# A two-layer graph network on one core: PE's signals given by drains instead of by matmuls

## What is computed

```python
# layer 0
scores = where(A != 0, -arange(N), -inf);  vals, idx = top_k(scores, 25)
agg = X[idx].max(over the 25);  agg = maximum(agg, 0) where degree <= 25
x = layernorm(x + relu(concat(x, agg) @ W + b))
# layer 1 (adjacency is 0/1, so one edge type is live)
h = x @ W1;  e_src, e_dst = h . a_src, h . a_dst          # per head
w = leaky_relu(e_src[i] + e_dst[j]) where adj, else -1e9
out = relu(softmax(w) @ h + bias) + h
x = layernorm(x + headwise_layernorm(out) * gamma + beta)
```

## Time and profile before

| | us |
|---|---|
| median of 3 runs (lowest to highest) | 6567.95 (6542.93 to 6576.8) |
| the profiled execution | 6569.77 |
| its span | 6568.0 |

### The profile page before, as it was taken

The page is one execution under the profiler, slowest core; times in us unless marked ns, Lnnn a source line. Parts: engine busy times, 40 slices in busy tenths (PEclk is TensorE's granted clock), DMA queues, the critical chain, the costliest instruction groups (busy, mean ns, idle before and its releaser), DMA issues.

```text
span 6568.0 us, 57561 instructions
## 1 busy us (share of the span) xinstructions
PE 3758.1 (57%) x12546; PEld 1690.9 (26%) x12546; DVE 3914.1 (60%) x12445; ACT 2183.1 (33%) x4674; POOL 3318.6 (51%) x3204
## 2 busy tenths in 40 slices
PE   1222456656556556556566556566556656555687
PEld 1111222322222222223222222222222222222232
DVE  4544565665665665666566556566556656656666
ACT  3333223333333333333333333333333333333212
POOL 4666555455455455455555545545545555554500
PEclk9555667677777777776777767777767777777888
DMA  4433333333333333333333333333333333333200
GB/s 125 122 115 115 105 100 105 103 100 109 105 99 110 99 105 106 107 96 105 100 106 109 100 102 108 100 105 104 104 98 105 103 102 107 104 102 98 78 21 26
DMA packets 264399, 658.75 MB, mean 100 GB/s; under 512 B 62161, under 2 KB 128978, under 8 KB 247762
## 3 DMA queue, kind: packets, MB, share of 16 engines
q0 software_dynamic: 153600, 419.64, 22.1%
q1 hardware_dynamic: 110546, 236.66, 10.3%
HBM read 605.73 MB, written 50.33 MB: 100 GB/s over the span
## 4 chain that ended last, share of the span: by engine, by line
another core or an unknown queue 26%; DVE 24%; PE 24%; issue 20%; ACT 5%; DVEq 1%; POOL 1%; DMA 0%; SPq 0%; ACTq 0%; POOLq 0%
PE acc L1253 11%; DVE uv L832 7%; PE pB L1221 5%; DVE rmax L851 3%; DVE top L719 3%; PE acc L1179 2%; DVE key_b L721 2%; PE pB L1222 1%; ACT raw L569 1%; PE pT L1153 1%; PE pB L1237 1%; DVE rmax L860 1%; DVE key_a L721 1%; DVE stf L953 1%
## 5 line engine op out<-in xcount | busy, mean ns | idle before, releaser
L492 POOL DMA_INDIRECT rows<-in_x_dram,idx x3200 | 3318.4, 1037 | 2891.7 <-DVE rmax L851 1693.3
L1253 PE MATMUL acc<-uv,hs 128*65 128x512 f32 x4096 | 2156.8, 683 | 172.5 <-ACT raw L569 171.5
L832 DVE SCALAR_TENSOR_TENSOR uv<-rq,qinv,maskT 128x512 f32<-128x512 f32 x2048 | 1504.4, 741 | 1175.5 <-remote 674.0
L1221 PE MATMUL pB<-w_sb,xaT 128*128 128x256 f32 x1024 | 443.9, 608 | 1305.6 <-DVE pad L734 794.6
L1253 PEld LDWEIGHTS acc<-uv,hs 128*65 128x65 f32 x4096 | 622.5, 159 | 1440.8 <-issue 1396.9
L634 ACT ACTIVATE xaT<-pA 128x512 f32<-128x512 f32 x128 | 76.4, 597 | 2071.6 <-remote 1788.3
L1221 PEld LDWEIGHTS pB<-w_sb,xaT 128*128 128x128 f32 x1024 | 300.6, 308 | 1469.0 <-issue 1012.8
L732 DVE SCALAR_TENSOR_TENSOR key_b<-pB,wordkey 128x128 f32<-128x128 f32 x128 | 36.7, 287 | 914.7 <-remote 834.0
L851 DVE TENSOR_TENSOR rmax<-rmax,rows 128x1280 f32<-128x1280 f32 x384 | 569.7, 1484 | 7.0 <-DMA rows<-in_x_dram,idx 4.4
L1231 PE MATMUL pA<-id,xh 128*128 128x128 f32 x256 | 81.6, 418 | 811.7 <-DVE xh L814 432.9
L643 ACT ACTIVATE x1T<-pA 128x256 f32<-128x256 f32 x128 | 49.2, 384 | 1089.5 <-PE pA L1231 979.2
(11 more groups left out here) (116 smaller groups left out, 4509.4 us busy)
## 6 DMA issues: line engine op xcount, KB each, us to landing
adj_sb<-in_adj_dram SPq DMA_DIRECT2D x128, 1024.0 KB
rows<-in_x_dram,idx POOLq DMA_INDIRECT x3200
xh_dram<-xh SPq DMA_DIRECT2D x128, 256.0 KB
xr<-xh_dram SPq DMA_DIRECT2D x64, 512.0 KB
xt<-in_x_dram SPq DMA_DIRECT2D x128, 128.0 KB
out_dram<-xr SPq DMA_DIRECT2D x32, 512.0 KB, 2.9
w_sb<-in_L_gnn_W_dram SPq DMA_DIRECT2D x1, 512.0 KB
wcat<-in_L_gnn_W_dram SPq DMA_DIRECT2D x2, 128.0 KB
```

The source lines that it names most:

```text
L492: nc.gpsimd.indirect_dma_start(rows[:, c, r * C:(r + 1) * C], None, x_rows, bass.IndirectOffsetOnAxis(ap=idx[u][:, k:k + 1], axis=0)).then ...
L832: stt = nc.vector.scalar_tensor_tensor(uv[k][:, i, :], rq[i][:], inv, m, ALU.max, ALU.mult)
L1221: nc.tensor.matmul(p_lin, xaT[:, c, :], w0_sb[:, c, :], start=(c == 0), stop=False)
L1253: last = nc.tensor.matmul(acc[i][0:HW, :], hs[:, (1 - quad.par) * JT + jt, h, :], uv[k][:, i, :], start=(jt == 0), stop=(jt == JT - 1))
```

## The change

Nine signals of PE's loops move. Where the last matmul of a group incremented the group's semaphore, now a drain instruction stands behind it and increments it. Matmuls, their order and all waits stay. The signal of the small check at the program's end (L1291) and the branch behind it are unchanged.

```diff
--- before.py
+++ after.py
@@ -1150,8 +1150,8 @@
                         pe.wait_ge(s_ring, v)
                     for j in range(HALF):
                         jt = hf * HALF + j
-                        last = nc.tensor.transpose(pT[hf][:, j * P:(j + 1) * P], mask_sb[:, jt * P:(jt + 1) * P], id16[:])
-                    last.then_inc(s_T, 1)
+                        nc.tensor.transpose(pT[hf][:, j * P:(j + 1) * P], mask_sb[:, jt * P:(jt + 1) * P], id16[:])
+                    pe.drain().then_inc(s_T, 1)
 
             def pack_words(quad, u, g_of):
 
@@ -1164,8 +1164,8 @@
                 for v in quad.reach(lambda q: QT * q + u + g_of - FRONT):
                     pe.wait_ge(s_proj, v)
                 for jt in range(JT):
-                    last = nc.tensor.matmul(p_key[:, jt * WPT:(jt + 1) * WPT], stage[:, jt, :], pack[:], start=True, stop=True)
-                last.then_inc(s_key, 1)
+                    nc.tensor.matmul(p_key[:, jt * WPT:(jt + 1) * WPT], stage[:, jt, :], pack[:], start=True, stop=True)
+                pe.drain().then_inc(s_key, 1)
 
             def back(quad, pair):
 
@@ -1176,9 +1176,9 @@
                 for i in range(QT):
                     for h in range(PAIR):
                         at = (i % 2 * PAIR + h) * HW
-                        last = nc.tensor.matmul(acc[i // 2][:, at:at + HW], sT[:, h, i * P:(i + 1) * P],
+                        nc.tensor.matmul(acc[i // 2][:, at:at + HW], sT[:, h, i * P:(i + 1) * P],
                                                 backmat[:, PAIR * pair + h, :], start=True, stop=True)
-                last.then_inc(s_back, 1)
+                pe.drain().then_inc(s_back, 1)
 
             def broadcast(quad, pair):
 
@@ -1188,9 +1188,9 @@
                     pe.sem_inc(s_go["pe"], 1)
                 block = (quad.q - BQ) % BQ * IB
                 for i in range(PAIR):
-                    last = nc.tensor.matmul(rq[i][:], headsel[:, PAIR * pair + i, :],
+                    nc.tensor.matmul(rq[i][:], headsel[:, PAIR * pair + i, :],
                                             er[0:HEADS, bass.ds((1 - quad.par) * N + block, IB)], start=True, stop=True)
-                last.then_inc(s_rq, 1)
+                pe.drain().then_inc(s_rq, 1)
 
             def transpose_xa(quad, u):
 
@@ -1205,8 +1205,8 @@
                     pe.wait_ge(s_proj, v)
                 for c in range(4):
                     src = (xt[p] if c < 2 else agg)[:, c % 2 * P:(c % 2 + 1) * P]
-                    last = nc.tensor.transpose(pA[:, c * P:(c + 1) * P], src, id32[:])
-                last.then_inc(s_xaT, 1)
+                    nc.tensor.transpose(pA[:, c * P:(c + 1) * P], src, id32[:])
+                pe.drain().then_inc(s_xaT, 1)
 
             def product0(quad, u):
 
@@ -1219,7 +1219,8 @@
                     pe.wait_ge(s_xaE, v)
                 for c in range(4):
                     nc.tensor.matmul(p_lin, xaT[:, c, :], w0_sb[:, c, :], start=(c == 0), stop=False)
-                nc.tensor.matmul(p_lin, ones_row[:], b0_sb[:], start=False, stop=True).then_inc(s_lin, 1)
+                nc.tensor.matmul(p_lin, ones_row[:], b0_sb[:], start=False, stop=True)
+                pe.drain().then_inc(s_lin, 1)
 
             def product1(quad, u):
 
@@ -1228,16 +1229,16 @@
                 for v in quad.reach(lambda q: QT * q + u):
                     pe.wait_ge(s_x1, v)
                 for c in range(2):
-                    last = nc.tensor.transpose(p_x1T[:, c * P:(c + 1) * P], xh[p][:, 0, c * P:(c + 1) * P], id32[:])
-                last.then_inc(s_x1T, 1)
+                    nc.tensor.transpose(p_x1T[:, c * P:(c + 1) * P], xh[p][:, 0, c * P:(c + 1) * P], id32[:])
+                pe.drain().then_inc(s_x1T, 1)
 
                 for v in quad.reach(lambda q: QT * q + u):
                     pe.wait_ge(s_x1E, v)
                 for c in range(2):
                     nc.tensor.matmul(p_h, x1T[:, c, :], wcat[:, c, :], start=(c == 0), stop=(c == 1))
                 for c in range(2):
-                    last = nc.tensor.matmul(p_es, wcat[:, c, C:C + HEADS], x1T[:, c, :], start=(c == 0), stop=(c == 1))
-                last.then_inc(s_h, 1)
+                    nc.tensor.matmul(p_es, wcat[:, c, C:C + HEADS], x1T[:, c, :], start=(c == 0), stop=(c == 1))
+                pe.drain().then_inc(s_h, 1)
 
             def attend(quad, u, a, b):
 
@@ -1250,9 +1251,9 @@
                         pe.wait_ge(s_u, v)
                     for i in range(PAIR):
                         h = PAIR * pair + i
-                        last = nc.tensor.matmul(acc[i][0:HW, :], hs[:, (1 - quad.par) * JT + jt, h, :], uv[k][:, i, :],
+                        nc.tensor.matmul(acc[i][0:HW, :], hs[:, (1 - quad.par) * JT + jt, h, :], uv[k][:, i, :],
                                                 start=(jt == 0), stop=(jt == JT - 1))
-                    last.then_inc(s_pe, 1)
+                    pe.drain().then_inc(s_pe, 1)
 
             def step(quad, u):
                 if quad.on(u, QT * BQ):
```

## The result

The changed kernel takes 7318.34 us (median of 4, 7287.37 to 7382.77) against 6572.38 us of the kernel before: ratio 1.113, 95% interval 1.102 to 1.125. It is 746 us slower where 569 us of gain were forecast. Two later pairs of the same two kernels gave 1.112 (1.109 to 1.115) and 1.115 (1.108 to 1.122). The execution profiled took 7348.81 us, span 7346.9.

What follows compares the result with a forecast made beforehand. No engine was the bound; PE's matmul signals were taken as held while POOL's gathers run. Held tiles 515 us plus free tiles 54 gave 569 us off 6569.77: 6000 us, range 5720 to 6780.

Steps and rivals of the forecast that it cites:

- If PE's signals come at once: In a held tile, ACT gets the transposes and PE starts product0 at 3019.8 instead of 3031.98: gain 12.2 us.
- held tile: Tile whose PE signals wait out POOL's gathers: 9.2 us gained on average, 6.2 after ACT's charge, times 83: 515 us.
- the drains' own price: What each drain costs PE, through waiting for its own end: 0.30 us taken, ends 0.05 and 0.60.
- free tile of a quad: One tile in four without the hole: L1179's signal 4.4 us earlier, less 2.4 for drains: 2.0 us, 54 over 27 quads.
- rival 2: The drain is let go no sooner than the matmul's signal; hole stays, drains add 165 us: 6735 us; chance 0.34.
- PE goes on with four more units in the hole: PE's work continuing during a held tile's hole, cited as evidence against rival 2; no size given.
- ACT's charge: 3.0 us per held tile for ACT's own signals being partly held; at 6 us the time is 6250, at none 5750.
- the third rival: PE's signals come, ACT's go out at the gathers' end: product0 0.9 us earlier, 25 us gained, 6595 us; chance 0.10.
- The sign I named: Forecast right if L634 starts within a microsecond of the last L1208 in all tiles.
- Rival 2's sign: From the first held tile on, L634 would still start 14 us behind L1208.
- the wait of L634 for "remote": Sign of being right: ACT's wait at its copy of the transposes falls from 1677.6 us to a few hundred.
- the period of a tile: Sign of being right: time per row tile falls from 49.5 us to about 44.

Runs made afterwards that it cites:

- before_again: The kernel before, unedited, run again in a holding place: 6573.11 us, ratio 0.998.
- after_again: The changed kernel, unedited, run again in a holding place: ratio 1.112 (1.109 to 1.115) against the kernel before.
- before_key_drain: The kernel before with only the key product's signal (s_key) given by a drain, in a free place: 5228.52 us, ratio 1.025.

## Why the prediction was wrong

**The step that failed** is "If PE's signals come at once", the 12.2 us gained in a held tile, and with it 83 x 6.2 = 515 us and the 54 us of the free tiles. No drain gets out of the hold: the key's stands 12.05 us at the median in a holding place and 0.52 in a free one. I read this so: what is held is not a message that another sender could bring; PE's work itself is not counted as done. The Trainium skill, "PSUM — Partial Sum Buffer", section "Engine vs sequencer instructions", has the drain wait until the engine is fully idle; the runs agree, with these two numbers. That the sequencer pushes the increment itself (the Trainium skill, "Perfetto Trace Analysis", section "Sequencer-only Instruction (DRAIN, etc)") is no help, since it does so only behind that wait. I had used the second rule to speak for the signal's early leave, and gave the first 0.34.

Beside it a term was too small, the drains' own price. The prediction charged the free tile of a quad 2.4 us for eight drains of 0.30, and rival 2 charged 165 us in all. In a free place, where nothing is held, the change costs 515 us, 3.7 us a tile by the table.

**The second rival had the mechanism and not the price.** It said 165 us, up to 330 with dear drains; measured were 740 to 746. It let PE's four units stay in the hole and counted the drains behind it. But a drain that waits also stops PE. In the held tile of kind the medians (table's tiles, before_again and after_again) are: before, the key's signal comes after 16.2 us, L634 after 22.4; after, PE is let go after 15.6 us and L634 starts after 28.8. PE is let go some 7 us earlier than the transposes' signal came, but 13.2 us now come behind it: three units, their drains, and the transposes. Part of that is standing again, as in the tile shown above (0.58 and 1.98 us); in the earlier trace rows units and transposes took 8.25 us (3007.99 to 3016.24). By the table, 5.2 us of the tile's 6.0 more lie between the key product and L634. I had written down the fact that settles it, "PE goes on with four more units in the hole", as evidence against the rival; it was its price.

**A drain's price.** Taken 0.30 us, ends 0.05 and 0.60; measured 0.42 from unit to unit. What it does to the time depends on where it stands: 0.04 us each for the ten outside the stretch, 0.99 for the key's alone, in a free place. The share by the clock (78 of its 124 us) was no term of mine. I had said of the clock only that a shorter hole would leave more of it high. Behind the stand the clock is low: by windows, the unit at 3016.18 of after and the one at 3027.88:

```profile
3016.18:3019.85 3.67, 3.67 (x4) 0.75 (x4) 0.12 (x1) 0.00 (x0) 2.83 (x3) 0.50 0.36 107
3027.88:3029.81 1.93, 1.92 (x4) 0.46 (x4) 0.77 (x2) 1.93 (x2) 0.00 (x0) 1.00 0.00 0
```

The same four matmuls take 3.67 us at half clock (1.2 GHz), right behind 14.64 us of standing, and 1.93 at full clock (2.4 GHz). Not all of it is new: behind the key product of the earlier trace rows the clock was 0.50 too (3008.13 to 3011.80). What the change adds is, in the mean of 100 tiles, 1.4 us a tile: units 4, 5 and 6 last 3.11, 2.57 and 1.88 us before and 3.62, 3.04 and 2.31 after.

**The free tile of a quad** was to gain 2.0 us. By the medians of the kind, key end to L634 went from 8.3 to 12.3 us: the hold of 3 us there, which was hidden, now stops PE too (it goes on 3.0 us behind the key product's end, where it had gone on 0.14 us ahead of it).

**ACT's charge** of 3.0 us and the third rival were never tried by the change, as PE's signals did not come free first.

**The sign I named was a bad one.** Right, it said, if L634 "starts within a microsecond of the last L1208": it does, in the tile shown 0.06 us behind it, and the kernel is 11% slower. Rival 2's sign was no better: L634 was to start 14 us behind L1208, and it doesn't. Both measured the signal from an instruction that the change itself moves. And the wait of L634 for "remote" is gone, as the prediction asked, but only because it now stands under PEq (2521 us). Measured from the key product's end they would have told at once; the other sign named, the period of a tile (44 us forecast, 56.0 found), did.

**What stays open** is the cause of the hold. Three groups met none, with the same program, and the kernels that change the store of xh fell only there, so they tell nothing of it. That the gathers begin or end it was not tried. It rests on times: in before_again L634 starts 4.1 to 4.7 us behind the start of the run's last gather in each of 72 held tiles (of the 25th to the 120th), as it did in the earlier trace rows. But the same gathers run in a free place and hold nothing there, and the key's signal comes some 6 us ahead of L634 at the median, so "until the run of gathers is over" doesn't hold for every signal. Why the key's drain costs so much less beside the others was not traced further than the table.

## What to carry to other kernels

A drain is not a cheap way to give a signal: it makes the engine wait for all that it has in flight, so whatever delays the end of one group delays all that is queued behind it. Where a wait hides work of the same engine, price the work that would leave the cover before asking how much sooner the signal might come, and measure a hole from an event that the change can't move. In this kernel a drain was nearly free where PE waits next anyway (0.04 us), and dearest right behind the short key product, which follows a wait (0.99 us, where nothing is held).

## What the hardware showed that was not expected

The same program, 6572 to 6593 us in one kind of place and 5102 to 5105 in the other, with every run of a group alike: 29% that no row of the kernel's own work accounts for. Engines' instructions are about as long in both (POOL's gathers 1036 and 1060 ns in the mean, L1253 683 and 669). What differs is when PE's ends are seen, and the tile, 11.5 us in the mean (48.6 against 37.1). In the holding places the trace also has few of the gathers' landings (semaphore increments, 16 for each of the 3200 gathers): 14,227 of 51,200 in before_again against 50,881 in before_key_drain. Whether this comes from the same cause isn't shown. A prediction that rests on such a hole should be told apart by place before it is trusted.
